# Two-layer decoder: the expert stage with four items in flight instead of two, heads in 64-row groups, and a table of turns for each lane

## The reference

```python
gate_logits = x.mean(axis=1) @ gate_w.T + gate_b
_, top_idx = jax.lax.top_k(gate_logits, K)               # K = 2 of E = 4
gate_weights = jax.nn.softmax(gate_logits, axis=-1)
...
def _encoder_layer(x, iw, ib, ow, ob, l1w, l1b, l2w, l2b, n1w, n1b, n2w, n2b):
    qkv = x @ iw.T + ib                                   # 16 heads of 16
    scores = jnp.einsum('bhqd,bhkd->bhqk', q, k) / scale
    attn = jax.nn.softmax(scores, axis=-1)
    o = jnp.einsum('bhqk,bhkd->bhqd', attn, v)...
    x = _layernorm(x + o @ ow.T + ob, n1w, n1b)
    ff = jax.nn.relu(x @ l1w.T + l1b) @ l2w.T + l2b       # 256 -> 1024 -> 256
    return _layernorm(x + ff, n2w, n2b)
```

## Time and profile before

| | |
|---|---|
| median of three runs | 4390.45 us |
| the profiled execution, its own time | 4404.57 us |
| its span | 4402.9 us |
| TensorE matmuls busy | 3745.0 us (85%), 35399 instructions |
| VectorE, ScalarE, GpSimd busy | 1952.9 (44%), 1446.5 (33%), 402.8 us (9%) |
| mean granted TensorE clock | 0.896 of full |
| stage 1, stage 2, expert stage, from about | 0, 1310 and 3058 us |

### The profile page before, as it was taken

How to read it: one execution, slowest core, us unless ns; L and a number is a source line. 1 busy time by engine, 2 the same in 40 slices (tenths; PEclk the granted TensorE clock), 3 DMA queues, 4 the chain that set the end, 5 groups by cost and what they waited for, 6 DMA issues and landing times. The chain is left out here.

```text
span 4402.9 us, 86449 instructions
## 1 busy us (share of the span) xinstructions
PE 3745.0 (85%) x35399; PEld 2818.8 (64%) x35399; DVE 1952.9 (44%) x5596; ACT 1446.5 (33%) x3267; POOL 402.8 (9%) x456
## 2 busy tenths in 40 slices
PE   6999999999688888888888888885788888888887
PEld 4777777777555555555565555563576777776666
DVE  3555555554244444443434444442354445444444
ACT  1333333332133333333333333331233333333333
POOL 1111111111000000000000000000010101101001
PEclk8999999999688888888888888896898999999898
DMA  1000000000100000000000000000101000001100
GB/s 67 11 14 11 11 14 11 12 13 6 69 10 15 16 16 16 16 16 16 16 11 14 16 16 16 16 11 23 63 13 45 10 12 13 11 12 39 51 13 10
DMA packets 62648, 86.99 MB, mean 20 GB/s; under 512 B 7602, under 2 KB 59442, under 8 KB 61506
## 3 DMA queue, kind: packets, MB, share of 16 engines
q1 hardware_dynamic: 54178, 75.73, 5.6%
q0 software_dynamic: 8224, 7.36, 1.5%
HBM read 64.38 MB, written 18.37 MB: 19 GB/s over the span
## 5 line engine op out<-in xcount | busy, mean ns | idle before, releaser
L1200 DVE TENSOR_TENSOR PX<-PX,pps 112x256 f32<-112x256 f32 x96 | 40.4, 421 | 529.6 <-PE pps L895 294.1
L1492 PE MATMUL bps<-BZT,wexp 128*128 128x112 f32 x2048 | 264.9, 284 | 0.9 <-ACT BZT L1625 0.9
L1575 PE MATMUL bps<-wexp,BHT 128*112 128x256 f32 x1024 | 259.3, 385 | 0.0
L632 POOL TENSOR_TENSOR rstd<-var,nhalf 112x1 f32<-112x1 f32 (+1 forms) x96 | 177.0, 1844 | 896.8 <-DVE var L551 540.2
L1492 PEld LDWEIGHTS bps<-BZT,wexp 128*128 128x128 f32 x2048 | 245.4, 196 | 15.9 <-ACT BZT L1625 1.2
L1302 POOL TENSOR_TENSOR Prstd<-Pvar,nhalf 112x1 f32<-112x1 f32 x128 | 69.1, 548 | 1844.0 <-DVE Pvar L1179 1844.0
L1108 ACT ACTIVATE PPT<-pps,mcol 125x896 f32<-125x896 f32 x192 | 186.3, 1005 | 132.4 <-PE pps L985 132.0
L1270 DVE CUSTOM_DVE_ANT_0 PON<-pps,PMR 112x375 f32<-112x375 f32 x256 | 130.0, 544 | 198.6 <-PE pps L968 197.5
L1750 DVE TENSOR_TENSOR BX<-BZ,bps 112x256 f32<-112x256 f32 x64 | 27.0, 421 | 403.0 <-PE bps L1575 403.0
L1632 ACT ACTIVATE BHT<-bps,wexp 128x112 f32<-128x112 f32 x512 | 152.8, 350 | 135.2 <-PE bps L1492 135.2
L1575 PEld LDWEIGHTS bps<-wexp,BHT 128*112 128x112 f32 x1024 | 166.3, 177 | 44.3 <-issue 18.4
(11 more groups left out here) (315 smaller groups left out, 8174.6 us busy)
## 6 DMA issues: line engine op xcount, KB each, us to landing
PCX<-in_ctx SPq DMA_DIRECT2D x32, 375.0 KB
wexp<-in_we SPq DMA_DIRECT2D x5, 2304.0 KB, 9.9
BXIN<-xmid SPq DMA_DIRECT2D x64, 112.0 KB, 2.0
out<-BY POOLq DMA_DIRECT2D x64, 112.0 KB, 2.9
wa_sb<-in_wa SPq DMA_DIRECT2D x1, 4736.0 KB, 15.1
wexp<-in_we SPq DMA_DIRECT2D x5, 777.0 KB, 4.4
XIN<-in_x SPq DMA_DIRECT2D x32, 112.0 KB, 2.1
CX<-in_ctx SPq DMA_DIRECT2D x32, 112.0 KB, 2.0
```

Of the source, the lines that this page charges most:

```text
L632: g.tensor_tensor(rstd[s][:, 0:n], var[s][:, 0:n], nhalf[0:T, 0:n], ALU.pow).then_inc(rstd_ready[s], 1)
L1492: m = mm(bk[:, j * T:(j + 1) * T], wt[:, c, n0 + j * 128:n0 + (j + 1) * 128], rhs[:, c, :], start=(c == 0), stop=(c == 1))
L1575: m = mm(b3[0:T, 0:D], HT[s][:, mt, :], W(s, "l2", FT)[:, mt, :], start=(mt == 0), stop=(mt == FT - 1))
```

## The change

Stages 1 and 2 stay as they are, in the same order. In the expert stage:

- Four lanes of 16 items take the place of two slots of 32, with two PSUM banks each. Each lane has its own weights and row parameters, so four sets are loaded at the start. SP loads the first parts and rows of lanes 3, 2, 1, 0, then the second parts in the same order, and then releases the other engines.
- The queries are masked for groups of 64 rows (4 heads), so two groups stand in the array side by side and write two banks. Scores, maxima, and exponentials go in two halves of 8 heads.
- Buffers are shared (`ZT` is `XT`, `OT` is `KT`, `OS` is in `QM`, `HT`, `ON`, `Z`, `ZN` are in `PT`), the hidden layer goes in two halves of 512.
- Each lane has its own table of turns, and the leads are given by a table (0, 264, 500, 764).

```diff
+    "lead3": (0, 264, 500, 764),
...
+    "pe3": ((0, 44, 204, 242, 269, 342, 477, 510, 549, 694, 733, 760, 828, 859, 859, 898, 904,),
...
-            local = turn + s * SPAN // n
+            local = turn + lead[s]
...
-            PS = [phase.enter_context(nc.psum_tensor(f"bps{s}", [128, 4, 512], F32)) for s in SLOTS]
-            bank = [[PS[s][:, b, :] for b in range(4)] for s in SLOTS]
-            wexp, rexp = two("wexp", [128, NWE]), two("rexp", [T, NRE])
+            PS = [phase.enter_context(nc.psum_tensor(f"bps{s}", [128, 2, 512], F32)) for s in LANES]
+            bank = [[PS[s][:, b, :] for b in range(2)] for s in LANES]
+            wexp, rexp = lanes("wexp", [128, NWE]), lanes("rexp", [T, NRE])
...
-                for s in SLOTS:
+                sp.wait_ge(route_dma, 16 * 9)
+                for s in reversed(LANES):
                     sp.wait_ge(x_in[s], 16)
                     sp.sem_clear(slot_sems[s]).then_inc(go_last[s], 1)
-                    load_weights(s, 0)
+                    load_early(s, 0)
                     load_rows(s, 0)
+                for s in reversed(LANES):
+                    load_late(s, 0)
                 sp.sem_inc(routed, 1)
...
-                    for e in range(4):
-                        for j in range(4):
-                            r = slice(32 * j, 32 * j + 32)
-                            m = mm(bank[s][j][0:T, e * T:(e + 1) * T], QM[s][r, e // 2, e % 2, :], KT[s][r, e // 2, :], start=True, stop=True)
-                    m.then_inc(s_psum[s], 1)
+                    for c in range(C2):
+                        yield
+                        if c == 0:
+                            t.wait(masked_ready[s], 2)
+                            t.wait(vx_read[s])
+                        else:
+                            t.wait(mx_ready[s])
+                        for v in range(4):
+                            for i in range(2):
+                                m = mm(bank[s][i][0:T, v * T:(v + 1) * T], QM[s][side[i], c, v, :], KT[s][side[i], c, :], start=True, stop=True)
+                        m.then_inc(s_psum[s], 1)
...
+                    for c in range(C2):
+                        yield
+                        if c == 0:
+                            t.wait(mt_ready[s])
+                        else:
+                            t.wait(p_ready[s])
+                        for v in range(4):
+                            for i in range(2):
+                                mm(bank[s][i][0:T, v * T:(v + 1) * T], msel[side[i], 4 * c + v, :], MXT[s][side[i], :],
+                                   start=(v == 0), stop=False, skip_group_check=True)
+                        for i in range(2):
+                            m = mm(bank[s][i][0:T, 0:QW], KT[s][side[i], c, :], QM[s][side[i], c, :, :], start=False, stop=True, skip_group_check=True)
+                        m.then_inc(st_psum[s], 1)
...
-                    A(PT[s][:, :, :], PS[s][0:T, :, 0:QW], ACT.Exp, scale=0.25).then_inc(p_ready[s], 1)
+                    for c in range(C2):
+                        yield
+                        t.wait(st_psum[s])
+                        A(PT[s][0:T, 8 * c:8 * c + 8, :].rearrange("p (i v) q -> p i (v q)", i=2), PS[s][0:T, :, 0:QW],
+                          ACT.Exp, scale=0.25).then_inc(p_ready[s], 1)
```

More of the change, by code:

```diff
@@ L97, in __init__, with run_slots @@
         self.n, self.last = n, last
-def run_slots(eng, lanes, count, batch, turns):
-    n = len(lanes)
-    at, runs = Place([0] * n), [None] * n
+def run_slots(eng, lanes, count, batch, turns, lead):
+    at, runs = Place([0] * len(lanes)), [None] * len(lanes)
     def work(s, turn):
-        while runs[s][1] < len(turns) and turns[runs[s][1]] <= turn:
+        while runs[s][1] < len(turns[s]) and turns[s][runs[s][1]] <= turn:
             next(runs[s][0], None)
@@ L120, in run_slots @@
     with eng.Fori(0, count - 1) as i:
-        at.n = [i] * n
+        at.n = [i] * len(lanes)
         for turn in range(SPAN):
             for s in lanes:
-                local = (turn + s * SPAN // n) % SPAN
+                local = (turn + lead[s]) % SPAN
                 if local == 0:
-                    at.n = [i + 1 if k == s and s else at.n[k] for k in lanes]
+                    at.n = [i + 1 if k == s and lead[s] else at.n[k] for k in lanes]
                     runs[s] = [batch(s, at), 0]
                 work(s, local)
-    at.n, at.last = [count - 1] * n, True
+    at.n, at.last = [count - 1] * len(lanes), True
     for turn in range(SPAN):
         for s in lanes:
-            local = turn + s * SPAN // n
+            local = turn + lead[s]
             if local == 0:
@@ L1361, in build @@
             onesq = sa("onesq", [B, B])
[L1363 to L1377 removed]
+            XIN, X, Y = lanes("XIN", [T, D]), lanes("X", [T, D]), lanes("Y", [T, D])
+            XT, KT = lanes("XT", [128, C2, T]), lanes("KT", [128, C2, T])
+            QM = lanes("QM", [128, C2, 4, T])
+            V32 = lanes("V32", [T, H, 32])
+            PT = lanes("PT", [128, H, T])
+            MXB, MXT = lanes("MXB", [T, 128], BF16), lanes("MXT", [128, T], BF16)
+            mx, rec = lanes("mx", [T, H]), lanes("rec", [T, H])
+            st6, mv, var, rstd = lanes("st6", [T, 6]), lanes("mv", [T, 2]), lanes("var", [T, 1]), lanes("rstd", [T, 1])
+            msel = csel
+            ZT, OT = XT, KT
+            upper = [PT[s][0:T, 8:16, :].rearrange("p h q -> p (h q)") for s in LANES]
+            ON, Z, ZN = ([a[:, k * D:(k + 1) * D] for a in upper] for k in range(3))
+            HT = [PT[s][:, 0:FT, :] for s in LANES]
+            OS = [QM[s][:, 0, :, :] for s in LANES]
+            onehot = ON[0][0:B, 0:E * NI].rearrange("p (e n) -> p e n", e=E)
+            listf, listi = sa("listf", [3, NI]), sa("listi", [2, NI], I32)
             def W(s, name, c):
@@ L1409, in change @@
                 def change(s, n):
-                    old = sp.value_load(items[0:1, bass.ds(n + (NI + s * (B + 1)), 1)], min_val=-1, max_val=E - 1)
-                    new = sp.value_load(items[0:1, bass.ds(n + (NI + s * (B + 1) + 1), 1)], min_val=0, max_val=E - 1)
+                    old = sp.value_load(items[0:1, bass.ds(n + (NI + s * (share + 1)), 1)], min_val=-1, max_val=E - 1)
+                    new = sp.value_load(items[0:1, bass.ds(n + (NI + s * (share + 1) + 1), 1)], min_val=0, max_val=E - 1)
@@ L1422, in load_weights, with load_late @@
                     with sp.Else():
                         sp.sem_inc(c_in[s], 16)
+                    sp.nop()
+                def load_late(s, n):
+                    old, new = change(s, n)
+                    with sp.If(old != new):
+                        sp.dma_start(wexp[s][:, early:NWE], we[bass.ds(new, 1), :, early:NWE].rearrange("a p n -> (a p) n")).then_inc(late_in[s], 16)
+                    with sp.Else():
                         sp.sem_inc(late_in[s], 16)
@@ L1654, in _ @@
                 v.memset(onesq[:, :], 1.0)
+                half_rows = ident.rearrange("p (i r) -> p r i", i=2)
+                step(v.tensor_reduce(msum[:, 0:16], half_rows[:, 0:16, :], AX_X, ALU.add))
+                step(v.tensor_tensor(msum[:, 16:24], msum[:, 0:8], msum[:, 8:16], ALU.add))
+                step(v.tensor_scalar(msel[:, :, :], msum[:, 16:24].unsqueeze(2).to_broadcast((128, 8, T)), -1.0, None, ALU.mult))
+                dve.wait_ge(route_dma, 16 * 2)
+                dve.wait_ge(added, 16)
                 v.tensor_copy(vals[:, :, 1], bidx[:, 1:1 + E])
```

273 lines of the change are left out of this document (125 added, 148 removed), and 34 rows, old and new, of the table TURNS.

## The result

The changed kernel takes 4266.29 us (median of 4 runs, 4258.35 to 4270.81), the kernel before 4391.16 in the same comparison: a ratio of 0.9716, 95% interval 0.9699 to 0.9733. The profiled execution took 4269.0 us with a span of 4267.0.

The account below looks back on a forecast made before the run. TensorE bounds the expert stage, busy 1086 of 1270 us at a mean clock of 0.92. The terms -137 + 16 + 8 + 12 + 6 = -95 us take 4390.45 to 4295 us; whole range 4260 to 4395.

Parts of the forecast that it names:

- The likeliest case: The forecast itself for the new expert stage: 4295 us, own range 4260 to 4340, chance 0.64.
- the two losses it named: In the expert stage's loop, TensorE's idle time (15%) and a clock not always full (mean 0.92).
- 64 items in the loop's rhythm: Expert stage loop: each item takes 17.84 us at full clock instead of 19.98, -137 us over 64 items.
- changes of expert: Three waits for new rows when a lane changes expert: half of some 31 us stays, +16 us (0 to 31).
- start, to the first scores: Expert stage start: release some 19 us later, but lane 3's loads have landed by then, +8 us (0 to 18).
- head and tail: More work stands ahead of and behind the loop; half of 27 us ahead counted exposed, +12 us (0 to 30).
- tight waits: Waits covered by only 0.1 us (exponential to second half, ZN to hidden layer, K to V): +6 us.
- the four holes: TensorE idle before transposes of OS, BON and ZN and before the output projection: 2.53 us an item, all closed.
- Four lanes can close the holes: Taken from stage 1, whose four lanes leave nothing idle inside a pass: holes close in the expert stage, -2.53 us an item.
- The loop too long: Rival: the new loop's 1368 records outgrow the instruction store, costing 83 us at back edges: 4378 us, chance 0.25.
- the two lengths the prediction left open: Store lengths at which the new loop would pay (1024), or the pass of 1868 could still lose its head (2048).
- Late copies: Rival: ScalarE and VectorE come late, opening holes that bring back the half clock; 4423 us at 2 us an item, chance 0.11.

Follow-up runs that it names:

- reversed old kernel: The kernel before, with SP asking for slot 1's loads ahead of slot 0's before the loop: 4380.65 us, ratio to the kernel before 0.9964.

## Why the prediction was right, and where its sizes were off

The likeliest case came: the two losses it named, holes and half clock, went, and nothing took their place. The medians are 124.9 us apart; the sum said -95. Its terms can only be measured in the profiled executions, whose spans are 4402.9 and 4267.0 us, 135.9 apart. These executions took 14.1 us more than the median named in the prediction and 2.7 more than the new one, so the table has 11 us more to account for than the medians moved. By the sum's own terms:

| term | predicted | measured | how |
|---|---|---|---|
| 64 items in the loop's rhythm | -137 | -164.5 | 64 x (19.98 - 17.41) |
| changes of expert | +16 | +14.5 | passes of 75.40, 69.99, 73.18, 74.50 less 69.65 each |
| start, to the first scores | +8 | +8.5 | 3102.99 to 3111.52 |
| head and tail | +12 | +5.6 | what is left of the span |
| tight waits | +6 | 0 | none among TensorE's waits in the loop; ten passes equal to 0.02 us |

- **The item was mis-sized.** 17.84 was taken and 17.41 measured, 27.5 of the 41 us missed. From start to start over a pass, the scores take 1.85 us an item for 1.94 predicted, the transposed scores 1.75 for 1.88, the broadcasts 0.47 for 0.60; together 0.35 of the 0.43. Each price was the distance to the next row in stage 1, or a choice between two bounds, and each lay on the dear side. A half's broadcasts took 0.24 us: above the 0.15 of the 32-row ones, below the 0.30 that was taken. The doubling from 32 to 64 rows by which 0.30 was argued held for the scores (1.85 for 0.98) but not for them. All three together are 4.07 us an item where the old scores, broadcasts and transposed scores took 0.98 + 1.20, so the 64-row groups cost 1.9 us an item, 121 us in all, of what four lanes bring. The 0.08 left of the 0.43 were not traced.
- **Holes and clock** were right: the four holes are gone, the loop is busy 98.9% at 0.99. The 1.45 us between 18.53 and 19.98 were split rightly too: 0.99 is the clock and 0.46 the changes of expert. So of the 2.57 us an item, 1.12 are holes and tails less the dearer rows, 0.99 the clock, and 0.46 the changes, of which half comes back in the next term. "Four lanes can close the holes" needs a table that fits: with another one they don't (4622.56 us).
- **Changes of expert.** The old cost was taken as some 31 us and was 29.6, and half of it stayed. The reason was right only in part: of 9.5 us of holes the rows, which the prediction named, stand behind 5.5 and the weights, which it did not name, behind 3.9; with the rows out of the way TensorE waits 11.6 us for the weights. That the sum came within 2 us of the "half" that was taken is partly luck, since no row gave it.
- **Start.** The size was right, and the mechanism but for one point: the old start waited for slot 1's loads queued last, as the reversed old kernel shows, but 7.60 us of that were for its weights and 4.95 behind its rows, where the prediction named the rows alone.
- **Head and tail.** Too dear. From TensorE's first transposes to the loop's first row it is 29.2 us (3103.41 to 3132.57). The rows between, at the prices they have in the loop, make 19.2 us of work, not the 27 that were taken, and 10 us are lost (3.3 in holes, the rest at the slow clock) where half of 27 was counted. The tail, from the last mark of the loop at 4190.41 us, takes 76.6 us for 51.5 us of work at the loop's prices: 11 lie behind TensorE's last matmul, as they did before, and 14 are lost ahead of it, where holes reappear with fewer lanes, the longest 4.00 us before the last transposes of ZN. What the old head and tail lost was not worked out in this way, so +5.6 is only the rest of the sum.
- **Tight waits.** The 6 us were an allowance with no row behind it, and none came.
- **The loop too long (0.25)** did not happen. A loop that is too long does pay as described, but this one has 1389 records and the end lies between 1645 and 1885. Of the two lengths the prediction left open, 1024 and one near 2048, the first is out, and a pass of 1885 or 1901 pays although it is below 2048. Why was not tested.
- **Late copies (0.11)** did not happen, and the place was well named: 0.49 us more there open a hole of 0.28. The clause that each such hole brings the half clock back was wrong at this size.

## What to carry to other kernels

Count how long TensorE is idle in short chains that no other work covers, and what clock it gets there; more items in flight took away both here, but only in an order in which the pieces interlock: the same lanes with a table that did not fit lost more than the whole gain. Count the clock by itself: it was 0.99 of the 2.57 us an item here. Count also what more lanes cost, here 1.9 us an item for the narrower split of the banks, and whether a better order alone would do; that was not run. Where one queue asks for all first loads, release the engines as soon as the first consumer's loads are asked for and put its loads first; that was worth 18 us here and costs a move of a few lines. Before a wait is taken away, see whether another runs beside it, and what the new request stands ahead of on its queue.

## What the runs showed of the hardware

- A loop of 1645 instruction records on TensorE fetches no packet in any pass; one of 1885 or 1901 fetches 9 to 11 in every pass and stalls 3.3 to 4.4 us at its back edge. The end lies between.
- Semaphore clears in fours between TensorE's matmuls cost next to nothing (256 for 0.4 us). From 8 to 12 in a row, 256 more cost some 27 us a pass, with 10 packets fetched in both.
- Four exponentials of 80 columns, 239 ns each by the trace, behind each other delay the next by 0.49 us, not by 0.96.
- Holes of 0.28 us, twice in a pass of 70 us, leave the granted clock at 1.00; holes of 16 us in all in a pass of 92 go with 0.92. Holes of 4.7 to 5.1 us in a pass of two items of the old loop went with 0.91, 0.96 or 1.00 in different passes.
- SyncE issues a load that it chooses from the item list every 2.0 us (12 requests from 3080.57 to 3103.04 us in the changed kernel), so where it releases the others among its requests decides their start.
